# Keys by tokens through a transposing DMA instead of TensorE, in a fused attention and tree layer

## The reference, cut to what matters

```
xn = layernorm(x)
Q = elu(xn @ Wq + bq) + 1 ;  K = elu(xn @ Wk + bk) + 1 ;  V = xn @ Wv + bv      # 16 heads of 64
for every token:  KV += outer(k, v) ;  Ks += k ;  out = (q @ KV) / (q . Ks + 1e-6)
attn = out @ Wo + bo
gate = sigmoid((xn @ tree_Wq.T) @ routers.T) ;  leaf_prob = product of gates or 1 - gates along each path
tree = (leaf_prob @ leaf_values) @ Wout_w.T + Wout_b
y = x + attn + tree
```

## Time and profile before

| | |
|---|---|
| runs | 1273.91, 1275.14, 1279.89 us; median 1275.14 |
| profiled execution | 1273.15 us, span 1271.4 us |
| TensorE busy | 1244.6 us (98% of the span) |
| VectorE, ScalarE, GpSimd busy | 64%, 49%, 29% |
| mean granted TensorE clock | 0.997 |

### The profile page before, as it was taken

How to read it: one execution, slowest core, us unless ns; L and a number is a source line. 1 busy time by engine, 2 the same in 40 slices (tenths; PEclk the granted TensorE clock), 3 DMA queues, 4 the chain that set the end, 5 groups by cost and what they waited for, 6 DMA issues and landing times.

```text
span 1271.4 us, 48688 instructions
## 1 busy us (share of the span) xinstructions
PE 1244.6 (98%) x22173; PEld 1105.0 (87%) x22173; DVE 810.3 (64%) x2186; ACT 622.4 (49%) x1007; POOL 374.3 (29%) x590
## 2 busy tenths in 40 slices
PE   5899999999999999999999999999999999999997
PEld 5789888898988989889898988989889898898986
DVE  4675766757576574765757666575765758657473
ACT  4563654536446363653636445364553636536361
POOL 3424232132421413223142321324214132231320
PEclk9899999999999999999999999999999999999999
DMA  6000001000000000001000010000000000000000
GB/s 223 19 3 19 19 2 35 3 18 20 10 28 3 19 19 10 28 3 36 2 19 19 3 35 3 19 20 10 28 3 19 19 18 20 2 19 3 19 3 18
DMA packets 21597, 25.91 MB, mean 20 GB/s; under 512 B 1025, under 2 KB 19728, under 8 KB 21392
## 3 DMA queue, kind: packets, MB, share of 16 engines
q1 hardware_dynamic: 21392, 22.82, 5.5%
HBM read 14.43 MB, written 8.39 MB: 18 GB/s over the span
## 4 chain that ended last, share of the span: by engine, by line
PE 97%; DVE 1%; ACT 1%; DMA 1%; SPq 0%; issue 0%; DVEq 0%
PE s_pair L655 25%; PE w_pair L655 20%; PE o_pair L667 9%; PE s_pair L667 9%; PE o_pair L765 6%; PE kv_pair L740 5%; PE o_pair L779 5%; PE s_pair L729 5%; PE w_pair L709 4%; PE w_pair L702 4%; PE w_pair L689 3%; DMA ffn_tok<-in_L_ffn_Wout_w_dram 1%; DVE snaps L585 0%; SPq L267 0%; PE o_pair L655 0%; ACT ex L407 0%
## 5 line engine op out<-in xcount | busy, mean ns | idle before, releaser
L329 POOL TENSOR_SCALAR_AFFINE_SELECT aT<-aT 64x512 f32<-64x512 f32 x256 | 167.6, 655 | 833.0 <-ACT aT L434 824.7
L655 PE MATMUL w_pair<-xnT,wk 128*128 128x512 f32 x768 | 205.7, 403 | 0.7 <-ACT k_tok L420 0.7
L655 PE MATMUL s_pair<-xnT,wq 128*128 128x512 f32 x756 | 194.0, 392 | 0.0
L434 ACT ACTIVATE aT<-s_pair 128x512 f32<-128x512 f32 x128 | 76.4, 597 | 238.3 <-PE s_pair L729 238.3
L585 DVE TENSOR_TENSOR snaps<-kv_pair,snaps 128x65 f32<-128x65 f32 x768 | 173.3, 226 | 26.4
L520 DVE SCALAR_TENSOR_TENSOR kT<-w_pair,bias_one,ex 128x512 f32<-128x512 f32 x128 | 96.2, 751 | 122.7 <-ACT ex L410 122.6
L655 PEld LDWEIGHTS s_pair<-xnT,wq 128*128 128x128 f32 x756 | 142.1, 188 | 31.4
L655 PE MATMUL s_pair<-wv,xnT 128*128 128x512 f32 x648 | 168.7, 395 | 0.0
L410 ACT ACTIVATE ex<-ex 128x512 f32<-128x512 f32 x256 | 161.8, 632 | 8.1
L407 ACT ACTIVATE ex<-w_pair,neg_bias 128x512 f32<-128x512 f32 x130 | 89.5, 689 | 148.5 <-PE w_pair L655 148.5
L655 PEld LDWEIGHTS w_pair<-xnT,wk 128*128 128x128 f32 x768 | 136.1, 188 | 26.6 <-ACT k_tok L420 1.0
(11 more groups left out here) (105 smaller groups left out, 1953.7 us busy)
## 6 DMA issues: line engine op xcount, KB each, us to landing
x_in<-in_L_attn_x_dram SPq DMA_DIRECT2D x16, 512.0 KB, 3.9
out_dram<-y_buf SPq DMA_DIRECT2D x32, 256.0 KB, 2.1
stage<-in_L_attn_Wv_dram SPq DMA_DIRECT2D x2, 512.0 KB, 8.0
stage<-in_L_attn_Wk_dram SPq DMA_DIRECT2D x2, 512.0 KB, 9.6
stage<-in_L_attn_Wq_dram SPq DMA_DIRECT2D x2, 512.0 KB, 10.8
stage<-in_L_attn_Wo_dram SPq DMA_DIRECT2D x2, 512.0 KB, 9.1
bv_all<-in_L_attn_bv_dram SPq DMA_DIRECT2D x1, 512.0 KB, 8.6
ffn_tok<-in_L_ffn_Wq_dram SPq DMA_DIRECT2D x1, 256.0 KB
```

Source lines behind the costliest of these rows:

```text
L329: pool.affine_select(out=part, in_=part, compare_op=ALU.is_ge, fill=0.0, base=0, pattern=[[0, 2 * CH], [1, D]], channel_multiplier=-1).the ...
L434: act.activation(aT[:, n % 2].rearrange("p h c q -> p h (c q)"), s_pair[:, :, 0:CH * D], ACT.Copy).then_inc(s_copied, 1)
L655: last = pe.matmul(dst, l, r, start=i == 0, stop=i == len(steps) - 1)
```

## The change

The keys by tokens of units 2 to 127 are no longer made by TensorE's transposes and ScalarE's copy. GpSimd (`take_apart`) splits `kT` into two planes of 16 bits, the low and the high halves of all words (`k_planes`). SP issues one transposing DMA of both planes to `k_turned` (`turn_keys`), 128 x 1024 elements of 16 bits. VectorE (`put_together`) interleaves the two turned planes into `k_tok`, between its last step of the keys of unit n + 3 and its last step of the queries of unit n + 2. The keys are filled three units ahead in place of two, the queries still two. TensorE waits for `put_together(n + 2)` (`k_whole`) in the middle of `oT` of unit n. With p of 7 `oT` follows `Q` and the two `y` fills follow each other. SP's list is ordered by units: the stores of a block stand at the start of the next one, the load of `x` at p of 2.

```diff
 def unit_fills(g, p, blocks):
-    ahead = divmod(n + 2, PAIRS) if n + 2 < blocks * PAIRS else None
+    keys = divmod(n + 3, PAIRS) if n + 3 < blocks * PAIRS else None
+    queries = divmod(n + 2, PAIRS) if n + 2 < blocks * PAIRS else None
...
-    if ahead:
-        fills += [(("K", ahead[1], ahead[0]), W0), (("Q", ahead[1], ahead[0]), S0)]
+    if keys:
+        fills.append((("K", keys[1], keys[0]), W0))
+    if queries:
+        fills.append((("Q", queries[1], queries[0]), S0))
     fills += [(name, S1) for name in tail]
+    fills.append((("oT", p, g), W1))
     if p == PAIRS - 1:
-        fills += [(("oT", p, g), W1), (("y", 0, g), O1)]
-    if ahead:
-        fills.append((("kT", ahead[1], ahead[0]), W0))
-    fills.append((("y", 1, g), S1) if p == PAIRS - 1 else (("oT", p, g), W1))
+        fills += [(("y", 0, g), O1), (("y", 1, g), S1)]
     return fills
 # SyncE
+            def turn_keys(m):
+                sp.wait_ge(k_apart, m - 1)
+                if m > 2:
+                    sp.wait_ge(k_whole, m - 2)
+                sp.dma_start_transpose(k_turned[:, :, :], k_planes[:, :, :].rearrange("p s t -> p (s t)"))\
+                  .then_inc(k_turned_in, 16)
+            turn_keys(2)
+            for n in range(UNITS):
+                g, p = divmod(n, PAIRS)
+                if p == 0 and g:
+                    store(g - 1)
+                if n + 3 < UNITS:
+                    turn_keys(n + 3)
+                if p == 2 and g + 2 < BLOCKS:
+                    sp.wait_ge(x_consumed, g + 1)
+                    sp.dma_start(x_in[:, g % 2], x_rows[g + 2]).then_inc(x_loaded[g % 2], 16)
+            store(BLOCKS - 1)
 # GpSimd
+            def take_apart(m):
+                g, p = divmod(m, PAIRS)
+                pool.wait_ge(drained[bank_of["K", p, g]], count_of["K", p, g])
+                if m > 2:
+                    pool.wait_ge(k_turned_in, 16 * (m - 2))
+                pool.tensor_copy(k_planes[:, :, :], kT[:, m % 2].bitcast(U16).rearrange("p (t s) -> p s t", s=2))\
+                    .then_inc(k_apart, 1)
+                pool.wait_ge(k_apart, m - 1)
...
                 if n + 1 < UNITS:
                     mask(n + 1)
+                if n + 3 < UNITS:
+                    take_apart(n + 3)
 # VectorE
+            def put_together(m):
+                dve.wait_ge(k_turned_in, 16 * (m - 1))
+                dve.wait_ge(kv_filled, m)
+                dve.tensor_copy(k_tok[:, :, :].rearrange("p c f -> p (c f)").bitcast(U16)
+                               .rearrange("p (n s) -> p s n", s=2),
+                               k_turned[:, :, :].rearrange("p (s c) f -> p s (c f)", s=2)).then_inc(k_whole, 1)
...
                     if kind in "KQ":
+                        if kind == "Q":
+                            put_together(n + 2)
                         phi(name)
 # TensorE, in the fill of oT and ahead of the outer products
                         if c == 1 and g * PAIRS + i + 1 < UNITS:
                             until(a_masked, 2 * (g * PAIRS + i) + 4)
+                        if c == 2 and g * PAIRS + i + 2 < UNITS:
+                            until(k_whole, g * PAIRS + i + 1)
...
-                until_drained(("kT", p, g))
+                if n < 2:
+                    until_drained(("kT", p, g))
+                else:
+                    until(k_whole, n - 1)
```

More of the change, by code:

```diff
@@ L9 @@
 F32R = mybir.dt.float32r
+U16 = mybir.dt.uint16
 P = 128
@@ L150, in attention_and_tree_layer @@
         k_tok = sb("k_tok", [P, CH, P])
+        k_planes = sb("k_planes", [P, 2, TOK], U16)
+        k_turned = sb("k_turned", [P, 2 * CH, P], U16)
         aT = sb("aT", [P, 2, 2, CH, D])
@@ L183, in attention_and_tree_layer @@
         tree_cols = [xn[:, 0:2].rearrange("p c n -> p (c n)"), xn[:, 2:4].rearrange("p c n -> p (c n)"),
-                     k_tok[:, :, :].rearrange("p c n -> p (c n)")]
+                     k_tok[:, :, :].rearrange("p c f -> p (c f)")]
         leafvT, woutT, routersT = [t.rearrange("p (t n) -> p t n", t=2) for t in tree_cols]
@@ L226, in attention_and_tree_layer @@
         kv_filled = sem("kv_filled")
+        k_apart = sem("k_apart")
+        k_turned_in = sem("k_turned_in")
+        k_whole = sem("k_whole")
         sum_ready = sem("sum_ready")
@@ L282, in _, with store @@
             load("wo1")
[L284 to L287, removed]
+            def turn_keys(m):
[4 more added lines that the diff above has]
+                  .then_inc(k_turned_in, 16)
+            def store(g):
                 for i in range(2):
@@ L370, in _ @@
             pool.wait_ge(leaf_step, 1)
+            take_apart(2)
             for n in range(UNITS):
@@ L419, in copy_keys @@
                 act.wait_ge(filled[bank_of[name]], count_of[name])
-                act.activation(k_tok[:, :, :].rearrange("p c n -> p (c n)"), psum_of(name), ACT.Copy)\
+                act.activation(k_tok[:, :, :].rearrange("p c f -> p (c f)"), psum_of(name), ACT.Copy)\
                    .then_inc(drained[bank_of[name]], 1)
@@ L468, in _ @@
             copy_keys(("kT", 1, 0))
+            exponential(("K", 2, 0))
             for n in range(UNITS):
@@ L478, in _ @@
                         high_of_output(name)
-                    elif kind == "kT":
-                        copy_keys(name)
                     elif kind == "xT":
@@ L515, in phi @@
             def phi(name):
-                kind, p, _ = name
-                slot, dst = (0, kT) if kind == "K" else (1, qT)
+                kind, p, b = name
+                slot, dst = (0, kT[:, p % 2]) if kind == "K" else (1, qT[:, p % 2])
                 col = p + (PAIRS if kind == "K" else 0)
                 dve.wait_ge(exp_ready, exp_count[name])
-                dve.scalar_tensor_tensor(out=dst[:, p % 2], in0=psum_of(name), scalar=bias_one[:, col:col + 1],
+                dve.scalar_tensor_tensor(out=dst, in0=psum_of(name), scalar=bias_one[:, col:col + 1],
                                          in1=ex[:, slot], op0=ALU.add, op1=ALU.max)\
                    .then_inc(drained[bank_of[name]], 1)
+            def put_together(m):
[4 more added lines that the diff above has]
+                               k_turned[:, :, :].rearrange("p (s c) f -> p s (c f)", s=2)).then_inc(k_whole, 1)
             def values(name):
@@ L615, in _ @@
             phi(("Q", 1, 0))
+            phi(("K", 2, 0))
             for n in range(UNITS):
@@ L701, in fill @@
                     for c in range(CH):
-                        last = pe.transpose(dst[:, c * P:(c + 1) * P], kT[:, i % 2, c * P:(c + 1) * P], ident[:, :])
+                        last = pe.transpose(dst[:, c * P:(c + 1) * P], kT[:, i, c * P:(c + 1) * P], ident[:, :])
                 elif kind == "oT":
@@ L876, in _ @@
             fill(("kT", 1, 0))
+            fill(("K", 2, 0))
             until(split_lo_pool, len(LO_POOL))
```

4 lines of the change are left out of this document (1 added, 3 removed).

## The result

The changed kernel takes 1287.36 us in the median of 5 runs (1285.15 to 1290.63), the kernel before 1275.28 (1273.91 to 1279.89) beside it: 1.0090 times as long, with a 95% interval of 1.0065 to 1.0115. The forecast was 1283 us in a range of 1268 to 1356. The profiled execution took 1290.63 us, 1288.8 of it span, 17.4 us more than the span before.

A forecast was written before the change was run, and what follows sets the result against it. TensorE, busy 1244.6 of 1271.4 us, was taken to bound the kernel. 54 us saved and 62 us given back as waits make +7.9 on 1273.15; with the median 2 us above, 1283 us, range 1268 to 1356.

The forecast's parts named there:

- What is removed, 54 us: TensorE's key transposes in 126 units: 111 slots of 0.44 us and 15 of 0.36, 54 us less with no wait added.
- The copy's duration: VectorE's put_together copy of 1,024 16-bit elements: 0.69 us taken by bytes, 1.22 by elements kept as the other end.
- rival 1: VectorE's copy goes by elements and takes 1.22 us: +74 us, 1349 us in all; chance 0.25.
- rival 4: Not slower: VectorE's copy takes 0.406 us, shorter than its bytes at 4 a cycle: -5.7 us, 1269 us; chance 0.14.
- the prediction's slope: From 0.69 us up, the VectorE copy's duration counts 125 times in the kernel's added time.
- The waits: TensorE idle before oT's transposes, held by VectorE's copy: about 1.3 us at p of 2 and 6, 1.4 at p of 7.
- The sum: Whole kernel: 125 times the copy's duration, less 78.3 us; with 0.69 us this is +7.9 us.
- The covers: GpSimd's gates and levels at p of 7 start 3.2 us later, hidden behind the 7 us second output: 0 us.
- The transfer: The transposing DMA of 256 KB takes 2.1 to 3.9 us, with 6.0 us hidden in ordinary units: 0 us.
- Rival 3: The transposing DMA is late: at 8.0 us it adds +240 us over some 123 units, some 1520 us; chance 0.08.
- Rival 2: VectorE's copy and GpSimd's take_apart collide, the copy takes 2.27 us: +205 us, 1480 us; chance 0.07.

The follow-up runs named there:

- The moved copies: Changed kernel with put_together's copy moved earlier on VectorE: ahead of the values at p of 2 and 6 alone, 1249.39 us; ahead of the keys' last step at p of 7 alone, 1266.33.
- the plain transfer: Changed kernel with the DMA moving the planes as they stand, not transposed; copies, waits and places unchanged: 1284.83 us, 1.0077 of the kernel before.
- the run with two copies: Changed kernel with put_together's copy made twice, one after the other, into the same k_tok: 1490.56 us, 1.1671 of the kernel before.
- the one with take_apart first: Changed kernel with three small VectorE operations ahead of put_together's copy, so that GpSimd's take_apart starts first: 1418.85 us, 1.1116 of the kernel before.

## Why the prediction was right

The forecast was 4 us low, and its mechanism is the one that the profile and the runs show.

- **What is removed, 54 us.** Right within a tenth: with nearly every wait gone a block is 3.07 us shorter than before, with the whole of the added work in it, where the forecast's slots are 7 x 0.44 + 0.36 = 3.44.
- **The copy's duration, the term in doubt.** I took 0.69 us and kept 1.22; the record is 0.75 (0.73 at p of 2, 6 and 7). The rate of one 4-byte element a cycle, rival 1's basis, does not hold for this copy. The step of two elements, named as what speaks against rival 4, is just that: without it the copy takes 0.42 us and the kernel lands at 1269.58, where rival 4 had 1269. So the bytes, by which I chose 0.69, don't set the duration either: the same 2 KB take 0.42 us without the step. That the choice came within 0.06 us is in part luck, and at the prediction's slope those 0.06 us are 7 us.
- **The waits.** Forecast 1.3 us at p of 2 and 6, 1.4 at p of 7, none at the others; measured 1.21, 1.29, and some 0.05 at p of 1 (the unit has 7.34 us against the 7.29 of the forecast). The moved copies take them away one kind at a time: 38 and 21 us for 31 x 1.21 and 15 x 1.29.
- **The sum.** With c of 0.75 at p of 0, 1, 3, 4 and 5 and 0.73 at the rest it is +14.5 us; the medians differ by 12.1, the profiled spans by 17.4. Against the spans three parts are off. At p of 3 of the first block the kernel is 2.8 us behind where the terms say 0.2 (I had put 2 either way at the start): the third key is now filled ahead of the first unit (1.65 us at 43.09), and TensorE waits for the copy already at p of 0 (0.63 us) and for 1.37 us at p of 2. The clock is no reason there: both kernels had 6.8 us at 0.50 between 17 and 75 us. From there to p of 3 of the last block, 15 blocks on, the span grew by 12.5 us where the terms say 15.8: the units of p 2 and 6 grew by 0.89 where c of 0.73 gives 0.94, and those at p of 5 and 0 shrank by 0.47 and 0.41 where it gives 0.38. From p of 3 of the last block on it grew by 2.1 where the terms say -1.4. Some 1.1 of this is mis-sized: I wrote of the third unit there that it has no new key to wait for and gains 1.3 us. It has one: the copy of the last key stands there, behind a transfer issued at 1254.67 and landed only in time for 1259.51, TensorE waited 1.48 us, and the unit gained 0.5. The other 2.4 us lie at the very end, in the stretch at half clock shown above, of which the terms know nothing.
- **GpSimd.** take_apart's 1.05 us were right only beside no copy; 1.44 otherwise. The covers held: no chain runs through the levels or the inverse deviation.
- **The transfer.** Forecast 2.1 to 3.9 us, measured 4.2, with 5.7 us between take_apart's end (608.94) and the copy of an ordinary unit that follows (607.29 + 7.34): hidden, as the plain transfer shows. Its margin is 1.5 us, not the 2 to 4 that my numbers gave. Rival 3 was dear when made to happen, but at 1437 us and not 1520; the doubled transfer there took 7.3 us, not the 8.0 of the rival.
- **Rival 2** is real in kind, and I gave it a wrong price (c of 2.27; behind take_apart the copy takes 1.45 to 1.58). Of my two reasons against it the first is refuted: one operand doesn't spare the copy. The second, the head start, is what spares it; it is 0.21 us and not 0.1. GpSimd pays 0.4 us, in time that nobody waits for. With the order turned round the kernel takes 1419 us.

## What to carry to other kernels

A copy that takes work off the bounding engine must be placed by what stands ahead of it on its own queue, unit kind by unit kind: here moving it past one or two steps of 0.7 us in 46 of 125 units, with the same work, made the difference between 0.9% slower and 3.5% faster. Put a wait where the data is first read: the work between the two places (two transposes and 16 small products, and in every eighth unit the output rows) was worth 43 us. When two engines can block each other, look at which starts first in the trace; a shift of 0.2 us can move the price from an idle engine to the one that counts.

## What the runs showed of the hardware

- **VectorE's copy and GpSimd's don't run at once.** The one that starts second ends nearly its own length after the first one's end. GpSimd's copy, 1.04 us alone, takes 1.44 when it starts 0.21 us behind, and ends 0.90 after VectorE's. VectorE's, 0.75 us alone, takes 1.45 to 1.58 when it is behind, and ends 0.60 after GpSimd's. The Trainium skill (SBUF — State Buffer, Who interferes with whom) says that the first to issue holds the shared pair of ports for the whole instruction and the other stands still, and that order alone decides; these runs agree, with the numbers above, within the 0.15 us by which the ends come sooner.
- **The output's step halves a 16-bit copy's rate.** 1,024 elements took 0.75 us written with a step of two, 0.42 without. The Trainium skill (VectorE: DVE Perf Modes, What auto-detection actually checks) asks for 16-bit tensors with a step of one for its fastest copy; the two rows agree with that.
- **Waits can cost more than their length, by the clock.** In the changed kernel, with 48 waits of 1.2 to 1.4 us, the mean granted clock was 0.995. In the run with two copies it was 0.967: between the start and the last microseconds the clock fell to 0.50 in 27 places, each time 0.0 to 1.5 us behind a wait of 2.0 to 2.8 us; another 22 waits of 2.0 to 2.9 us had no fall behind them. Shorter waits are not safe for it: the one fall in the middle of the changed kernel, at 71.2 us, came 0.9 us behind a wait of 1.37. What is left of the sums there, 38 us in that run and 12 in the one with take_apart first (clock 0.987), has the size that the clock's mean gives (45 and 14); the clock was not tried by itself.
- **A transposing transfer is slower than a plain one of the same bytes** (4.2 against 2.5 us to landing for 256 KB within SBUF; 3.1 for the second of two made one after the other). Beside them x_in's 512 KB landed after 5.0 us, 4.2 with plain transfers, 3.9 before; but with each transposing transfer made twice it was 4.1, so their number alone doesn't set it. SyncE's issue of one took 1.23 us in the median, that of the plain one 0.47.
